# Centred gate weights and a one-hot matrix that carries the row scale, with five engine queues in a new order

## The chip, the cores and the metric

One NeuronCore of a Trainium2 chip runs the kernel. The time is the device time of one execution in microseconds, as the median of several runs. The profiled execution is one further run; its span goes from the first to the last instruction that the profiler shows.

## The reference

Four images of 512 tokens with 512 features go through two gated residual blocks. The first builds, from a 512 x 128 context, a similarity matrix of tokens, keeps in each row the values above the row's 153rd largest, and mixes the normalised input with it:

```
sim = einsum(Q, K) / (sqrt(d) * H)                  # 512 x 512 an image
threshold = top_k(sim, 153)[..., -1:]
A = sigmoid(sim) * (sim >= threshold)
A = (A + A^T) / 2
x = x + tanh(g_xattn) * ((1 - gamma) * layernorm(x) + gamma * A)
```

The second is a mixture of eight experts with two picks a token (gate, softmax over the picks, weights times alpha):

```
n = layernorm(x)
probs = softmax(n @ gate_w);  score, idx = top_k(probs, 2)
h = gelu(n @ fc1_w[e] + fc1_b[e]);  y = h @ fc2_w[e] + fc2_b[e]
x = x + tanh(g_ffn) * sum over the two picks of share * alpha[e] * y
```

Everything is float32. fc1_w and fc2_w are 8 x 512 x 512 each, 16 MB together.

## The kernel before

The program is written with explicit queues: each engine (SyncE for DMA, GpSimd, ScalarE, VectorE, TensorE) has a list of named steps, laid out by hand in one order, and semaphores between them. A queue runs strictly in its order, so a step that waits holds all steps behind it. Steps are named `step(b, t)` for image b and row tile t (128 rows, four an image), or `step(k, e)` for the rows of image k that went to expert e. Images are taken in the order 2, 0, 1, 3, and b counts in that order.

An image goes through these stages.

- Scores. TensorE turns the context (`turn_context`), multiplies by the folded Wq and Wk (`project`, L1596) and makes 512 x 512 scores (`scores`, L1600); ScalarE copies and scales them (`context`, `query`, `scores`).
- Threshold. VectorE takes mean and variance of each row of scores (`sim_stats`) and makes a first guess (`first_guess`, L1014). In three rounds ScalarE (`signs`) and for image 0 also VectorE (`count`) count the scores below the trial threshold, and VectorE moves the trial (`narrow`, L1040). Then `candidates` (ScalarE), `largest` and `threshold` (VectorE) find the value, and TensorE sums the flags in `prove`; VectorE reads the sum into a register in `prove` (L1107) and goes on.
- Mask and first block. ScalarE has made the sigmoid (`squash`, `halve`) and the normalised input (`affine_x`, L719, from `x_stats`, `x_var`, `x_scales` of VectorE and a power on GpSimd). VectorE masks (`mask`), adds (`total`), TensorE transposes the masked matrix (`adjacency`, L1616), VectorE adds that (`add`). `store_x1` of SyncE writes the sum out.
- Second norm and routing. VectorE takes the statistics (`x1_stats`, `x1_var_of`), GpSimd the power (`rstd_of_x1`), VectorE the bias (`norm_bias`) and the normalised rows (`norm`, L1168) into `ab`. TensorE transposes the raw sum (`turn`), ScalarE copies (`turned`), TensorE multiplies by the gate weights (`gate`, L1643) into `logit_ps`, a PSUM tile. `best_two` (L1174) takes off the mean times the column sums of the gate weights (`gate_sum`, from `sum_gate` and `keep_gate_sum`) into `logits`, finds the two largest and their numbers, and makes the one-hot `hot` and `member`. `rank` (TensorE), `shares` and `places` (VectorE) give each row its weights and its place in the lists of its experts.
- Dispatch. GpSimd writes the rows of `ab` to these places in DRAM by eight indirect DMAs an image (`scatter_rows`, L561). SyncE reads them back by expert (`load_rows`, L384, four DMAs each) and reads the rows' numbers and weights (`load_meta`, read by `targets` on VectorE). For the first two experts of image 0 the rows don't take that way: `norm_plain` (ScalarE, L732) makes the normalised rows, `one_hot` (VectorE, L1234) a matrix that picks them, `pick_rows` (TensorE, L1661) multiplies the two, `picked` (ScalarE, L740) copies the result.
- Experts. `turn_rows` (VectorE, L1300) transposes the read rows, `layer1` (TensorE, L1670) 64 or, in pairs of passes, 32 profiled matmuls, `gelu` (ScalarE), `layer2` (TensorE, L1698), `add_bias` (VectorE, L1316, with the row that `load_b2` brought), `weigh` (ScalarE) and `add_result` (GpSimd, L570), an indirect DMA that adds the rows into the output. One of these DMAs waits for the one before. The result rows lie in two buffers for images 0 to 2, so that `add_bias(m)` waits until m - 1 results have been added (`freed`). In the last image the lists are 160 long; the 32 rows behind 128 are done for four experts at once (`tails`, `spread_tokens`, `find_twins`, `merge`, `add_tails`).

TensorE has only one queue, in which the stages of the images are interleaved: scores and masks of image b + 1 and b + 2 stand between experts of image b. `keep_busy` (L1579) is filler, small matmuls whose result nobody reads; `busy_to_threshold` starts it when two tiles of `largest` are done. Weights come expert by expert, two MB each (`load_weights`, L316); two of the eight pairs come after the stores of image 0.

## Time and profile before

| | us |
|---|---|
| median of three runs | 364.29 |
| lowest and highest | 364.28, 367.03 |
| span of the profiled execution | 363.4 |
| TensorE busy in the span | 324.3 |
| VectorE busy | 200.7 |
| ScalarE busy | 165.0 |
| GpSimd busy | 100.1 |

The page of the profile gives busy times, the granted clock of TensorE by slices, the chain of work that ended last, and groups of instructions. The table by stage gives the same for any stretch. The list of waits says which instruction an engine stood before, and which engine and line released it. A timeline gives single or merged instructions: start, duration, engine, line, operation, output and inputs, and in brackets the idle time before and its releaser. Times count from the start of the span. A 128 x 512 instruction of VectorE or ScalarE that stands in a run is shown with some 0.7 us but starts about 0.6 us behind the one before.

### The profile page before, as it was taken

Reading aid. Unit: us, or ns where it says so; the run is one execution under the profiler, and the core shown is the slowest. Engines: PE = TensorE matmul, PEld = TensorE weight load, DVE = VectorE, ACT = ScalarE, POOL = GpSimd, SP = SyncE. Lnnn points to the kernel's source line nnn. Section 1 sums busy time; section 2 is a strip of 40 time slices with the busy share of each in tenths; the row PEclk is TensorE's granted clock in tenths of the full one; section 3 lists DMA queues with packets and bytes.
Section 4 is the critical chain, followed back from the end, with each engine's and each line's share of the span. In section 5 each row is a group of like instructions: output and inputs, shape, how many; then the busy total and the mean of one; then the engine's idle time right before and its main releaser. Section 6 shows DMA issues by size and latency. Waiting matters only on the chain.

```text
span 363.4 us, 6131 instructions
## 1 busy us (share of the span) xinstructions
PE 324.3 (89%) x1937; PEld 232.9 (64%) x1937; DVE 200.7 (55%) x697; ACT 165.0 (45%) x384; POOL 100.1 (28%) x141
## 2 busy tenths in 40 slices
PE   6906899779998999899999989999999999999960
PEld 4402667677764786678778576777785877577610
DVE  0488698887879777898886372636206112311010
ACT  2485515389996746256786222232222213132320
POOL 5001001361111357114307431331733111312031
PEclk9975699899999999999999999999999999999996
DMA  2999989977974696876627587744678854533253
GB/s 91 379 392 369 352 298 331 378 267 139 305 145 123 144 243 231 146 161 183 113 54 181 191 173 135 211 100 81 203 163 149 176 119 104 111 64 87 30 74 46
DMA packets 53636, 65.79 MB, mean 181 GB/s; under 512 B 9792, under 2 KB 28512, under 8 KB 53600
## 3 DMA queue, kind: packets, MB, share of 16 engines
q1 hardware_dynamic: 46144, 47.99, 43.7%
q0 software_dynamic: 7456, 17.37, 24.7%
q8 instruction: 16, 0.26, 0.3%
q14 instruction: 20, 0.16, 0.1%
HBM read 39.56 MB, written 25.78 MB: 180 GB/s over the span
## 4 chain that ended last, share of the span: by engine, by line
PE 50%; issue 18%; DVE 14%; DVEq 5%; DMA 5%; POOL 3%; POOLq 2%; ACT 2%; ACTq 0%
PE ps L1711 21%; PE ps L1684 13%; PE ps L1694 10%; DMA out_rows<-ab,dst 3%; PE ps L1647 2%; POOL xs_rows L566 2%; DMA meta<-xs_rows 2%; DVE top L1087 1%; DVE stats L1012 1%; PE ps L1607 1%; PE ps L1721 1%; PE ps L1627 1%; PE ps L1639 1%; POOLq L530 1%; DVEq L1086 1%
## 5 line engine op out<-in xcount | busy, mean ns | idle before, releaser
L1684 PEld LDWEIGHTS ps<-xgT_r,weights 128*128 128x128 f32 x768 | 87.8, 192 | 8.3 <-issue 6.7
L1684 PE MATMUL ps<-xgT_r,weights 128*128 128x128 f32 x768 | 89.6, 276 | 3.6 <-ACT xgT_r L743 2.0
L1711 PE MATMUL ps<-weights,act_r 128*128 128x512 f32 x192 | 86.3, 595 | 1.5 <-ACT act_r L766 1.5
L580 POOL DMA_INDIRECT out_rows<-ys,dst x24 | 37.9, 1578 | 115.2 <-ACT ys L773 70.0
L1711 PEld LDWEIGHTS ps<-weights,act_r 128*128 128x128 f32 x192 | 34.9, 190 | 38.4 <-issue 36.5
L766 ACT ACTIVATE act_r<-ps,b1T 128x128 f32<-128x128 f32 x96 | 27.1, 365 | 38.9 <-PE ps L1684 38.8
L1694 PEld LDWEIGHTS ps<-sim,weights 128*128 128x128 f32 x256 | 35.2, 190 | 1.9 <-issue 1.7
L566 POOL DMA_INDIRECT xs_rows<-ab,pos x32 | 31.9, 998 | 14.5 <-issue 9.1
L1694 PE MATMUL ps<-sim,weights 128*128 128x160 f32 x256 | 35.6, 299 | 0.0
L773 ACT ACTIVATE ys<-ys,meta 128x512 f32<-128x512 f32 x24 | 17.3, 719 | 31.3 <-DVE ys L1322 31.3
L1322 DVE TENSOR_TENSOR ys<-ps,b_r 128x512 f32<-128x512 f32 x24 | 16.5, 686 | 23.4 <-PE ps L1711 22.0
L1711 PE MATMUL ps<-weights,xb 128*128 128x512 f32 x64 | 28.1, 592 | 0.0
L1322 DVE TENSOR_TENSOR ab<-ps,b_r 128x512 f32<-128x512 f32 x10 | 6.9, 691 | 35.8 <-PE ps L1711 30.0
L692 ACT ACTIVATE ab<-sim,t_now 128x512 bf16<-128x512 f32 x36 | 25.5, 719 | 2.4 <-DVEq L1057 2.3
L580 POOL DMA_INDIRECT out_rows<-ab,dst x8 | 12.3, 1542 | 46.2 <-ACT ab L773 30.3
L1309 DVE STREAM_TRANSPOSE xgT_r<-xg_r 128x512 f32<-128x512 f32 x22 | 15.5, 707 | 12.9 <-PE ps L1684 11.9
L1607 PE MATMUL ps<-ctxT,qT 128*128 128x512 f32 x32 | 20.9, 782 | 0.7 <-ACT qT L677 0.7
L766 ACT ACTIVATE xb<-ps,b1T 128x160 f32<-128x160 f32 x32 | 10.0, 395 | 24.7 <-PE ps L1694 24.7
L1711 PEld LDWEIGHTS ps<-weights,xb 128*128 128x128 f32 x64 | 11.9, 190 | 13.4 <-issue 13.4
L1309 DVE STREAM_TRANSPOSE sim<-sim 128x640 f32<-128x640 f32 x8 | 6.8, 845 | 22.3 <-PE ps L1694 21.1
L1647 PEld LDWEIGHTS ps<-gate_w,x1T 128*128 128x128 f32 x128 | 15.7, 192 | 2.2 <-issue 1.4
L1582 PE MATMUL ps<-ones_b 128*128 128x128 bf16 x136 | 12.0, 260 | 5.5 <-DVE top L1087 3.0
(206 smaller groups left out, 419.0 us busy)
## 6 DMA issues: line engine op xcount, KB each, us to landing
weights<-in_L_ffn_fc_w SPq DMA_DIRECT2D x16, 1024.0 KB, 8.0
b_r<-in_L_ffn_fc_b SPq DMA_DIRECT2D x32, 256.0 KB, 4.1
xg_r<-xs_rows SPq DMA_DIRECT2D x88, 64.0 KB
xb<-in_x SPq DMA_DIRECT2D x4, 1024.0 KB, 7.1
out_rows<-xb SPq DMA_DIRECT2D x4, 1024.0 KB, 5.5
sim<-xs_rows SPq DMA_DIRECT2D x32, 80.0 KB
xs_rows<-weights SPq DMA_DIRECT2D x1, 2064.0 KB, 13.5
xs_rows<-weights SPq DMA_DIRECT2D x2, 516.0 KB, 5.9
```

The lines of the kernel that those rows point to most:

```text
L566: pool.indirect_dma_start(out=xs_rows, out_offset=bass.IndirectOffsetOnAxis(ap=pos[:, g:g + 1], axis=0), in_=ab[:, b % 2, t, :], in_offset ...
L580: pool.indirect_dma_start(out=out_rows, out_offset=bass.IndirectOffsetOnAxis(ap=dst[:, k % 2, e:e + 1], axis=0), in_=result_rows(m), in_of ...
L692: last = act.activation(junk(b, t), score_of(b, t), ACT.Sign, bias=t_now[:, i:i + 1], scale=-1.0, accum_out=cnt[:, i:i + 1])
L766: last = act.activation(to, at, ACT.Gelu, bias=b1T[:, e * IB + i:e * IB + i + 1])
L773: act.activation(result_rows(m), result_rows(m), ACT.Copy, scale=meta[:, k % 2, e, 3:4]).then_inc(ys_ok, 1)
L1309: dve.transpose(to, at.rearrange("p (s k i) -> p k s i", k=KB, i=QUAD)).then_inc(xgT_ok, 1)
L1322: dve.tensor_tensor(result_rows(m), ps[:, 2 + u, :], b2_r[:, u, :], ALU.add).then_inc(y_sb, 1)
L1607: pe.matmul(ps[:, SIDE_BANK + t % 2, :], qT[:, t * P:(t + 1) * P], ctxT[:], start=True, stop=True).then_inc(sim_ps, 1)
L1647: mm = pe.matmul(logit_ps[:, t, :], x1T[:, t % 2, k * P:(k + 1) * P], gate_w[:, k, :], start=(k == 0), stop=(k == KB - 1))
L1684: mm = pe.matmul(ps[:, n % 2, i * P:(i + 1) * P], weights[:, e, 0, h, i * P:(i + 1) * P], rows[:, h * P:(h + 1) * P], start=(h == 0), stop ...
L1694: mm = pe.matmul(at, weights[:, e, 0, h, i * P:(i + 1) * P], rows[:, h * LAST:(h + 1) * LAST], start=(h == 0), stop=(h == KB - 1))
L1711: mm = pe.matmul(ps[:, 2 + m % 2, :], rows, weights[:, e, 1, i, :], start=(i == 0), stop=(i == IB - 1))
```

## The change

Three edits of the arithmetic and a new order of all queues.

1. The gate weights are centred once: `centre_gate` on VectorE subtracts from each column of the gate weights its mean, from the sums that `sum_gate` made. `gate` then multiplies by `gate_c`, which takes the row mean off by itself, and `best_two` reads `logit_ps` directly. `gate_sum` and `logits` go.
2. `norm_plain` only subtracts the row mean, from the new `neg_mean`, and no longer waits for the scale.
3. `one_hot` multiplies the picking matrix by the row's scale (one over the standard deviation), so that `pick_rows` gives the normalised rows.
4. SyncE, GpSimd, ScalarE, VectorE and TensorE run their steps in another order. Two waits move or are new on TensorE (`m_sb` into `project`, `gate_ok` into `gate`), one on ScalarE (`mean_ok` for `bias_ok`).

The edits of the arithmetic, and the parts of the order that the prediction speaks of, queue by queue (SyncE, GpSimd, ScalarE, VectorE, TensorE):

```diff
-            load_b2(0, 1)
+            load_weights(6)
             store_x1(0)
             fill_pads()
-            load_weights(6)
             load_x(2)
-            load_weights(7)
+            load_b2(0, 1)
             load_meta(0)
             load_rows(0, 2)
             load_rows(0, 3)
             fill_ends()
             load_rows(0, 4)
+            load_rows(0, 5)
             load_b2(0, 2)
-            load_rows(0, 5)
             load_b2(0, 3)
-            load_rows(0, 6)
             load_b2(0, 4)
             store_x1(1)
             load_b2(0, 5)
+            load_rows(0, 6)
+            load_weights(7)
             load_rows(0, 7)
+            load_b2(0, 6)
             load_x(3)
-            load_b2(0, 6)
+            load_rows(1, 0)
+            load_rows(1, 1)
             load_b2(0, 7)
+            load_meta(1)
             load_b2(1, 0)
...
             load_b2(2, 6)
+            load_rows(3, 2)
             load_b2(2, 7)
-            load_meta(3)
-            for t in range(3):
-                load_rows(3, t)
             load_b2(3, 0)
             load_rows(3, 3)
+            load_rows(3, 4)
+            load_meta(3)
...
+            add_result(0, 0)
+            add_result(0, 1)
+            add_result(0, 2)
             rstd_of_x1(1)
             add_result(0, 3)
+            scatter_rows(1, 0)
+            scatter_rows(1, 1)
+            scatter_rows(1, 2)
             add_result(0, 4)
-            for t in range(BT):
-                scatter_rows(1, t)
+            scatter_rows(1, 3)
...
+            rstd_of_x1(3)
             add_result(1, 7)
             add_result(2, 0)
-            rstd_of_x1(3)
             add_result(2, 1)
+            scatter_rows(3, 0)
             add_result(2, 2)
+            scatter_rows(3, 1)
+            scatter_rows(3, 2)
+            scatter_rows(3, 3)
             add_result(2, 3)
-            for t in range(BT):
...
-                    act.wait_ge(bias_ok, 1)
+                    act.wait_ge(mean_ok, 1)
                     act.wait_ge(blank, 16)
                     act.wait_ge(sum_ps, 1)
-                act.activation(plain(t), xb[:, 0, t, :], ACT.Identity, scale=xn_scale[:, t:t + 1],
-                               bias=xn_bias[:, t:t + 1]).then_inc(plain_ok, 1)
+                act.activation(plain(t), xb[:, 0, t, :], ACT.Identity, bias=neg_mean[:, t:t + 1]).then_inc(plain_ok, 1)
...
-            scores(2, 2)
             scores(2, 3)
             context(3)
-            for t in range(BT):
-                affine_x(1, t)
-            query(3)
             signs(1, 0)
             picked(0)
             picked(1)
@@ -833,126 +853,140 @@
...
                 dve.drain().then_inc(x1_var, 1)
+                if b == 0:
+                    dve.tensor_scalar(neg_mean[:], mv1[:, :, 0], -1.0, None, ALU.mult).then_inc(mean_ok, 1)
...
                 for t in range(BT):
-                    dve.scalar_tensor_tensor(logits[:, t, :], gate_sum[:], mv1[:, t, 0:1], logit_ps[:, t, :], ALU.mult,
-                                             ALU.add)
+                    dve.max(out=best[:, t, :], in_=logit_ps[:, t, :])
                 dve.drain()
                 for t in range(BT):
-                    dve.max(out=best[:, t, :], in_=logits[:, t, :])
-                dve.drain()
-                for t in range(BT):
-                    dve.max_index(out=best_i[:, t, :], in_max=best[:, t, :], in_values=logits[:, t, :])
+                    dve.max_index(out=best_i[:, t, :], in_max=best[:, t, :], in_values=logit_ps[:, t, :])
...
-                    last = dve.tensor_scalar(xg_r[:, e, t * P:(t + 1) * P], place_no[:], chosen[:, t, e:e + 1], None,
-                                             ALU.is_equal)
+                    last = dve.tensor_scalar(xg_r[:, e, t * P:(t + 1) * P], place_no[:], chosen[:, t, e:e + 1],
+                                             xn_scale[:, t:t + 1], ALU.is_equal, ALU.mult)
...
-            def keep_gate_sum():
+            def centre_gate():
                 dve.wait_ge(sum_ps, 1)
-                dve.tensor_scalar(gate_sum[:], total_ps, -1.0, None, ALU.mult)
-
+                for k in range(KB):
+                    last = dve.scalar_tensor_tensor(gate_c[:, k, :], total_ps, -1.0 / D, gate_w[:, k, :], ALU.mult, ALU.add)
+                last.then_inc(gate_ok, 1)
+
+            x_stats(0, 0)
+            x_stats(0, 1)
+            x_stats(0, 2)
+            x_stats(0, 3)
+            x_var(0)
+            sim_stats(0, 0)
+            x_stats(1, 0)
             coefficients()
+            x_scales(0)
+            x_stats(1, 1)
+            sim_stats(0, 1)
+            sim_stats(0, 2)
+            sim_stats(0, 3)
+            centre_gate()
             first_guess(0)
-            keep_gate_sum()
             count(0, 0)
-            x_stats(0, 1)
             narrow(0, 0)
             count(0, 1)
-            x_stats(0, 2)
             narrow(0, 1)
             count(0, 2)
-            x_stats(0, 3)
-            x_var(0)
             narrow(0, 2)
-            x_scales(0)
-            x_stats(1, 0)
-            for t in range(BT):
-                largest(0, t)
-            x_stats(1, 1)
...
+            total(0, 0)
+            sim_stats(1, 2)
+            total(0, 1)
+            total(0, 2)
+            total(0, 3)
+            add(0, 0)
+            add(0, 1)
+            x_stats(1, 3)
+            add(0, 2)
+            add(0, 3)
+            x1_stats(0, 0)
+            x1_stats(0, 1)
+            x1_stats(0, 2)
+            x1_stats(0, 3)
+            sim_stats(1, 3)
+            first_guess(1)
             x1_var_of(0)
-            x_stats(1, 2)
-            x_stats(1, 3)
+            best_two(0)
             norm_bias(0)
             norm(0, 0)
             norm(0, 1)
-            best_two(0)
             norm(0, 2)
+            sim_stats(2, 0)
+            one_hot(0)
+            sim_stats(2, 1)
             norm(0, 3)
+            gaps(0)
             x_var(1)
-            sim_stats(1, 0)
...
-            sim_stats(1, 3)
-            first_guess(1)
-            for t in range(BT):
-                sim_stats(2, t)
             first_guess(2)
             narrow(1, 0)
-            for t in range(BT):
-                x_stats(2, t)
+            next_places(0)
+            x_stats(2, 0)
+            x_stats(2, 1)
+            narrow(1, 1)
+            x_stats(2, 2)
+            x_stats(2, 3)
             x_var(2)
-            narrow(1, 1)
             x_scales(2)
+            narrow(1, 2)
             targets(0)
             turn_rows(0, 2)
-            narrow(1, 2)
             add_bias(0)
+            add_bias(1)
             turn_rows(0, 3)
+            largest(1, 0)
...
             scores(1, 0)
             scores(1, 1)
+            turn_context(2)
             busy_to_threshold()
+            prove(0)
+            keep_busy(BUSY_MASK)
             scores(1, 2)
-            prove(0)
+            keep_busy(16)
             scores(1, 3)
-            keep_busy(BUSY_MASK)
-            project(2)
             adjacency(0, 0)
             adjacency(0, 1)
+            project(2)
+            turn_b1()
             turn_context(3)
-            keep_busy(16)
             adjacency(0, 2)
             adjacency(0, 3)
...
             pick_rows(0)
-            project(3)
             pick_rows(1)
             layer1(0, 0)
             layer1(0, 1)
             layer2(0, 0)
+            layer2(0, 1)
             layer1(0, 2)
-            layer2(0, 1)
+            project(3)
             layer1(0, 3)
             layer2(0, 2)
             prove(1)
+            layer2(0, 3)
             layer1(0, 4)
-            layer2(0, 3)
...
             layer2(0, 5)
             layer2(0, 6)
             prove(2)
+            scores(3, 2)
+            scores(3, 3)
             layer1(0, 7)
-            layer2(0, 7)
             adjacency(2, 0)
             adjacency(2, 1)
+            layer2(0, 7)
             layer1(1, 0)
             layer1(1, 1)
...
+            layer1(1, 6)
             layer1(1, 7)
             adjacency(3, 0)
+            layer2(1, 6)
             adjacency(3, 1)
-            layer1(2, 0)
             layer2(1, 7)
-            layer2(2, 0)
-            layer1(2, 1)
             adjacency(3, 2)
             adjacency(3, 3)
+            layer1(2, 0)
+            turn(3, 0)
+            layer1(2, 1)
...
-            layer1(2, 3)
+            layer1(2, 4)
             gate(3, 2)
             gate(3, 3)
+            layer2(2, 2)
             layer2(2, 3)
             rank(3)
...
             layer2(2, 6)
-            layer2(2, 7)
             layer1(3, 0)
             layer1(3, 1)
+            layer1(3, 2)
+            layer2(2, 7)
...
+            spread_tokens()
             tails(0)
-            spread_tokens()
-            layer1(3, 4)
+            layer1(3, 5)
             merge(0)
-            layer1(3, 5)
+            layer1(3, 6)
             layer2(3, 4)
             layer2(3, 5)
-            layer1(3, 6)
             layer1(3, 7)
             layer2(3, 6)
             layer2(3, 7)
```

## Rows read from the trace of the kernel before

**Rows 1.** The page, part 1 (busy us, share).
```profile
PE 324.3 (89%) x1937; PEld 232.9 (64%) x1937; DVE 200.7 (55%) x697; ACT 165.0 (45%) x384; POOL 100.1 (28%) x141
```

**Rows 2.** Table by stage: stretch, its length, busy us (instructions) by engine, clock.
```profile
107.00:150.00 43.00, 39.98 (x226) 27.05 (x225) 35.79 (x113) 26.36 (x60) 17.12 (x16) 1.00 0.68 172
...
150.00:230.00 80.00, 78.80 (x505) 60.19 (x504) 54.56 (x178) 39.91 (x99) 27.21 (x22) 1.00 0.66 147
```

**Rows 3.** TensorE's waits from 78 us: us in total, times, longest.
```profile
PE ps L1711 <- ACT act_r L766: 1.5, 2, 1.2
...
PE ps L1684 <- DVE xgT_r L1309: 1.2, 1, 1.2
...
PE ps L1627 <- DVE xb L1149: 1.0, 1, 1.0
```

**Rows 4.** Timeline of VectorE, image 0: start us, duration us, line, operation.
```profile
18.78 0.16 DVE L1025 SCALAR_TENSOR_TENSOR t_now<-dev,mv 128x4 f32<-128x4 f32 x1
...
20.89 0.69 DVE L992 BATCH_NORM_STATS2 statx<-xb 128x6 f32<-128x512 f32 x1
...
33.01 0.17 DVE L1079 COPY_PREDICATED t_now<-under,keep 128x4 f32<-128x4 int32 x1
...
59.32 0.62 DVE L1178 SCALAR_TENSOR_TENSOR logits<-gate_sum,mv,ps 128x8 f32<-128x8 f32 x4
...
60.02 0.37 DVE L1182 MAX8 best<-logits 128x8 f32<-128x8 f32 x4
...
65.84 0.87 DVE L1242 TENSOR_SCALAR xg_r<-place_no,chosen 128x128 f32<-128x128 f32 x4
...
69.35 0.17 DVE L1231 CAST pos<-pos_f 128x8 uint32<-128x8 f32 x1
```

**Rows 5.** Timeline of TensorE; last row from the chain that ended last.
```profile
37.49 4.02 PE L1582 MATMUL ps<-ones_b 128*128 128x128 bf16 x36 [3.00 <-DVE top L1087]
...
44.06 3.23 PE L1582 MATMUL ps<-ones_b 128*128 128x128 bf16 x48
...
66.77 1.23 PE L1666 MATMUL ps<-xg_r,act_r 128*128 128x128 f32 x4 [2.42 <-DVE xg_r L1242]
...
71.95 1.02 PE L1598 MATMUL ps<-ctxT,m_qk 128*128 128x512 f32 x2
...
78.56 7.38 PE L1684 MATMUL ps<-xgT_r,weights 128*128 128x128 f32 x64 [2.02 <-ACT xgT_r L743]
...
85.78 3.60 PE L1711 MATMUL ps<-weights,act_r 128*128 128x512 f32 x8
...
251.47 0.24 PE L1658 MATMUL ps<-member,ones_b 128*128 128x8 bf16 x4
...
279.84 8.69 PE ps L1694 x64
```

**Rows 6.** Table by stage, two short stretches: the granted clock is named after POOL's.
```profile
42.00:44.00 2.00, 2.00 (x6) 0.48 (x5) 0.65 (x2) 0.60 (x1) 0.00 (x0) 0.84 1.04 399
...
66.00:67.00 1.00, 0.23 (x1) 0.24 (x2) 0.99 (x7) 0.60 (x2) 0.00 (x0) 0.77 1.06 408
```

**Rows 7.** Timelines of ScalarE, GpSimd, SyncE and VectorE, in order of time.
```profile
71.48 2.93 ACT L722 ACTIVATE xb<-xb,xa_bias,xa_scale 128x512 f32<-128x512 f32 x4 [4.88 <-DVEq L1008]
...
130.74 1.57 POOL L580 DMA_INDIRECT out_rows<-ys,dst  x1 [4.95 <-ACT ys L773]
...
264.04 0.97 POOL L566 DMA_INDIRECT xs_rows<-ab,pos  x1 [0.30 <-issue]
...
268.31 0.38 SPq L377 DMA_DIRECT2D meta<-xs_rows  x1
...
278.17 0.85 DVE L1309 STREAM_TRANSPOSE sim<-sim 128x640 f32<-128x640 f32 x1 [1.02 <-DMA sim<-xs_rows]
...
345.21 1.54 POOL L580 DMA_INDIRECT out_rows<-ab,dst  x1 [8.50 <-ACT ab L773]
...
350.85 1.54 POOL L580 DMA_INDIRECT out_rows<-ab,dst  x1 [4.10 <-DMA out_rows<-ab,dst]
```

542 lines of the change are left out of this document (296 added, 246 removed).

## The prediction

> **What bounds the kernel now.** I read the page first, then the table by stage, then TensorE's waits, then the timelines of the five engines around each wait. TensorE is busy 89% of the span, but the mean hides two regimes [rows 1]. From 78.56 us, the first expert matmul of `layer1(0, 0)`, it has almost no idle time: 3.0 us of the 43 from 107 on and 1.2 of the 80 behind [rows 2]. What it waited for there is a short list: 1.5, 1.2 and 1.0 us [rows 3], and 2.0 at 78.56 itself, where ScalarE's `picked` came late [rows 5]. So the time is the start of `layer1(0, 0)`, plus TensorE's work behind it, which the change doesn't alter, plus some 4 us of waits, plus the tail. Before 78.56 TensorE mostly waits; the chain there runs through image 0's threshold search, mask, statistics, routing and one-hot matrices, nearly all on VectorE. A microsecond off that chain counts only until another queue, equally late, holds TensorE.
>
> **The small edits.** `best_two` loses four scalar_tensor_tensor instructions, 0.62 us in a run, and a drain, together 0.70 from the start of L1178 to that of L1182 [rows 4]. In return four MAX8 and four index searches read PSUM. No row has either with a PSUM source; the bounds are the 0.09 us step of the SBUF MAX8 and the 0.155 step of the PSUM-reading L1178. Eight times the difference is 0.5 us, so an image gains 0.2 to 0.7. I take 0.2, since L1178 is the nearest row: same shape, same source. With 0.7 all behind it would be 0.5 earlier. The Trainium skill, VectorE: DVE Perf Modes, section "The TRN2 errata", gives a PSUM source 62 cycles more than an SBUF one; eight instructions would be an estimated 0.5 us more. By the page the edit gains 0.2, not 0.7. The one-hot compare gains a second scalar operand (0.87 us for four, [rows 4]): nothing below, and 0.3 above if each cost as much as L1178's extra step. `norm_plain` waits for the mean instead of the scale and bias, and is no longer last: in the new order it ends near 64, before the one-hot matrix that the same matmuls need. `centre_gate` is four instructions like L1178, 0.6 us, in place of one small one, and stands ahead of the first trial threshold. The three new waits (on the gate sums, the mean and the centred weights) are for work that ends at least 2 us earlier in the layout below.
>
> **The front in the new order.** I laid the new queues out with the durations of the trace.
> - Threshold search. Before, the first trial was out at 18.94 and the last at 33.2 [rows 4]. Now four `x_stats`, `x_var`, three of them formerly between the rounds, `x_scales`, two of image 1 and `centre_gate` run ahead of it: the first trial comes near 21.7. Between the rounds only `count` and `narrow` remain, and each former `x_stats` there was 0.6 us [rows 4]: the last trial comes near 33.3. No gain, no loss.
> - Mask. `prove(0)` no longer stands behind a half-clock score matmul: 0.6 us earlier. One `sim_stats` and one `x_stats` put between `total` and `add` cost 1.2. The statistics of x1 start about 0.5 later than before.
> - Routing. `sim_stats(1, 3)` and `first_guess(1)` (2.2 us) stand ahead of `x1_var_of(0)`, so the mean is out near 59.0, later than before, but `best_two(0)` follows at once rather than after two `x_stats`, `norm_bias` and two `norm`. Members near 61.6. The matmuls that it reads (`gate`) end near 58.5, hidden behind the statistics.
> - One-hot matrices. `one_hot(0)` stands behind three `norm` and one `sim_stats` instead of two, two, an `x_var` and `gaps`: 65.3 against 66.7 [rows 4]. `one_hot(1)` ends near 68.5, and TensorE asks for it only at 70.5.
> - `pick_rows(0)` starts at 65.3 instead of 66.77 and I keep its 5.2 us, since it began at half clock after an idle stretch [rows 5, 6]; `project(3)`, 0.9 us in the pipeline [rows 5], no longer divides the two; `pick_rows(1)` follows: ends 74.1.
> - `picked(0)` on ScalarE stood behind four `affine_x(1, ..)` (2.9 us) that waited for VectorE until 71.5 [rows 7]. These are moved behind the first experts; `signs(1, 0)` finds its trial ready since 58, so both copies are done by 74.7.
>
> `layer1(0, 0)` then starts at 74.1 instead of 78.56 [rows 5]: 4.5 us. `project(3)` comes back after `layer1(0, 2)`: minus 0.9, so 3.6 us.
>
> **What holds TensorE next.** `layer2(0, 1)` now comes right behind `layer2(0, 0)`. Its GELU is behind `signs(1, 1)`, the table load, `gelu(0, 0)` and `signs(1, 2)`: near 85.0, wanted at 74.1 plus two `layer1` of 3.6 and a `layer2` of 3.45 (the starts 78.56 and 85.78, and 3.60 less the overlap [rows 5]), 84.75: 0.3 late. `layer1(0, 2)` needs `turn_rows(0, 2)`, which has been moved behind `narrow(1, 2)` (2.5 us); rows are written by the eight scatters of image 0, whose places come 1.1 later than the 69.5 of before [rows 4]. The transpose ends near 89.2, 0.8 after TensorE asks. Left: 2.5 us. Behind `layer1(0, 4)`, `adjacency(1, 2)` waits for `add(1, 0)`, which follows the four `halve` and two late `affine_x`: 1.7 us against 1.0 [rows 3] and two short ones, 0.5 together, before. Left: 2.3.
>
> **The middle.** Before, `layer2(0, 7)` waited 1.2 us for its GELU, TensorE paused 0.3 at a rank (part of the 3.0 of [rows 2]), and `layer1(2, 0)` waited 1.2 for its transpose [rows 3]. In the new order `scores(3, 2)`, `scores(3, 3)` and `adjacency(2, 0)` stand ahead of `layer2(0, 7)` and cover the first; `rank(1)` finds its members; `layer2(1, 7)`, `adjacency(3, 2)` and `(3, 3)`, 4.3 us, are new ahead of `layer1(2, 0)`; by the layout its rows are turned near 209.3 and TensorE asks near 211.4. All three go: 2.7 us. Lead 5.0. The b2 loads, `store_x1` and `load_x` are moved within SyncE's queue and land at least 2 us before their readers by the same laying out; `load_weights(7)` now goes out near 118, needed near 138; in return `load_x(2)` has no 2 MB ahead of it while DMA is full.
>
> **The last image.** `rank(3)` gets `layer1(2, 4)` (3.6 us) ahead of it, so with a lead of 5.0 it ends at 250.3 instead of 251.7 [rows 5]. Places take 1.15, eight scatters of 1.28 (start to start) 10.2, and `add_result(2, 2)`, which before stood behind all eight and now among them, 1.85: the last scatter ends near 263.2 (before 265.0), and SyncE, which went on at 268.3, goes on at 266.5 [rows 7]. It now issues rows ahead of the metadata: issue 2.0, landing 3.0 (as for the rows awaited at 278.17 [rows 7]), transpose 0.85: 272.4. TensorE asks at 279.84 [rows 5] less the 3.4 of `layer2(2, 7)`, which now stands behind, less 5.0: 271.4. With a landing of 2.5 or 3.0 that is 0.5 or 1.0 lost; I take 0.8. The tail is the same chain of accumulating DMAs behind `layer2(3, 6)`; with `layer1(3, 6)` moved ahead of `layer2(3, 4)` the adds of experts 4 and 5 just finish before that of 6 is ready (5.6 us each from issue to issue [rows 7], 11.2 for 4.35 + 2 x 3.45). No term.
>
> Sum against the profiled span: 363.4 - 4.5 + 0.9 + 1.1 + 0.2 - 2.7 + 0.8 = 359.2. The median of the runs is 0.9 above the span, which I carry along: 360.1.
>
> **Rivals.**
> - A, this forecast: 358.3 to 361.7. Chance 0.46, 0.36 of it under 360.65.
> - B, the front's gain comes but each wait saved in the middle returns elsewhere (a hand layout misses some): 364.3 - 2.3 + 0.8 = 362.8, up to 364.5. For it: every queue changes, and the experts have only two row buffers. Against: the idle times of VectorE in the middle are small but exist. Chance 0.22.
> - C, the late pieces near 85, 89, 110 and 271 are all on time: 364.3 - 3.6 - 2.7 - 1.5 = 356.5, to 358.3. Chance 0.14.
> - D, slower. On GpSimd three `scatter_rows(1, ..)` now stand before `add_result(0, 4)`, which before was issued at 130.74, ahead of them [rows 7]. It must wait for image 1's places (near 128.4), then 7.7 us of scatters, then 5.5 of its own: landed 141.6. `add_bias(6)` on VectorE waits for it and is reached near 143; behind it stands `turn_rows(1, 0)`, without which TensorE has nothing. Places later than 129.8 cost time one for one; over 5.6 us late the kernel is slower than before, and at 10 us late it takes 368.7. The same is laid out for images 2 and 3. Chance 0.10.
> - E, the clock. The fillers from 37.49 ran without a gap into the scores, and the granted clock rose from 1.2 to 2.4 GHz within 42 to 44 us [rows 5, 6]. Now `prove(0)` waits some 0.3 us after the fillers' end. If the rise goes late by the whole stretch to the turns, 48 fillers at the pace of the first 36 (0.11 us against 0.067 [rows 5]) cost 2.0 more, and scores, adjacency and projection about 2.3: 364.3. Chance 0.08. The Trainium skill, TensorE: Matmul & The Clock Gate, Part 1, has the throttled state as the default, which activity lifts. By that rule, with which the rise behind the fillers agrees, E is possible.
>
> **Numbers.** About 1% (3.64 us) is what a measurement can tell from no change. Faster by more: 0.36 + 0.14 = 0.50. Within: 0.10 + 0.22 + 0.08 = 0.40. Slower: 0.10. The range 356.5 to 364.5 leaves out D, the low end of C (0.04) and the high end of B and E (0.04).
>
> **What would show it.** Right: `layer1(0, 0)` within 1 us of 74.1; ScalarE no longer releasing it; small waits at 85 and 89 and one of 1 to 2 us at `adjacency(1, 2)`; no wait at `layer2(0, 7)` and `layer1(2, 0)`; `layer1(3, 0)` near 272; TensorE's last expert matmul some 4.2 us earlier. Wrong: a first trial later than 22, a wait of `ys` L1322 for a DMA, or a clock of 0.5 after 44 us.

## The result and the profile after

| | before | after |
|---|---|---|
| median of 4 runs, us | 364.91 | 371.59 |
| lowest and highest | 364.28, 367.03 | 368.83, 375.20 |
| profiled execution, its span | 363.4 | 367.8 |

The ratio is 1.0148, 95% interval [1.0100, 1.0196]: the kernel after is 1 to 2% slower. The ratio leaves out the run of 375.20 as a slow one, since it lies more than 1.5% above the fastest. The four runs of after have mean granted clocks of 0.960, 0.959, 0.934 and 0.950 in the order 368.83, 369.54, 373.63, 375.20 us, so the two slower ones had the lower clocks, though not in strict order. The trace below is that of the run of 369.54.

Busy times of the whole span, from the page of the profile after (in before: [rows 1]):

```profile
PE 322.6 (88%) x1937; PEld 231.9 (63%) x1937; DVE 197.2 (54%) x685; ACT 163.2 (44%) x384; POOL 101.3 (28%) x141
```

TensorE does the same work in 1.7 us less, since more of the front ran at full clock, yet the span is 4.4 us longer: the loss is idle time. (The clock of the front differs from run to run: the kernel before, profiled again as c0 below, has 325.1 us of work on TensorE where the first profile has 324.3.) Its longer waits from 74 us on, from the timeline of TensorE (start, duration, engine, line, operation, tiles; in brackets the idle time and its releaser; rows without a wait and three with 0.33 to 0.43 are left out):

```profile
74.42 7.31 PE L1765 MATMUL ps<-xgT_r,weights 128*128 128x128 f32 x64
83.29 3.70 PE L1792 MATMUL ps<-weights,act_r 128*128 128x512 f32 x8 [1.57 <-ACT act_r L778]
87.32 3.70 PE L1792 MATMUL ps<-weights,act_r 128*128 128x512 f32 x8 [0.33 <-ACT act_r L778]
92.26 3.81 PE L1765 MATMUL ps<-xgT_r,weights 128*128 128x128 f32 x32 [1.24 <-issue]
...
113.36 1.23 PE L1706 MATMUL ps<-ident,ab 128*128 128x128 f32 x8 [1.23 <-DVE xb L1183]
...
129.63 0.20 PE L1735 MATMUL ps<-member,before 128*128 128x8 bf16 x2 [0.31 <-DVEq L1228]
131.06 3.81 PE L1765 MATMUL ps<-xgT_r,weights 128*128 128x128 f32 x32 [0.93 <-issue]
...
153.66 7.41 PE L1765 MATMUL ps<-xgT_r,weights 128*128 128x128 f32 x64 [0.88 <-DVE xgT_r L1341]
...
188.88 1.06 PE L1728 MATMUL ps<-gate_c,x1T 128*128 128x8 f32 x8 [1.53 <-ACT x1T L743]
...
301.09 3.70 PE L1792 MATMUL ps<-weights,xb 128*128 128x512 f32 x8 [0.55 <-ACT xb L778]
```

With the three left out they make 9.7 us, where before had 2.0 at `layer1(0, 0)` [rows 5] and 4.2 behind it (the listed ones of [rows 3], one of them 0.23, and two more of 0.24 and 0.34). `layer1(0, 0)` starts at 74.42: the front's gain came. By `layer2(0, 2)` TensorE is 0.5 us later than before. Behind `gate(2, 3)` (188.88) the clock fell; the table by stage (length, busy time of each engine with counts, granted clock, DMA share, GB/s):

```profile
188.00:190.70 2.70, 1.82 (x16) 1.82 (x17) 2.04 (x10) 2.25 (x6) 0.00 (x0) 1.00 0.81 151
190.80:194.10 3.30, 3.30 (x18) 3.30 (x17) 2.76 (x13) 1.14 (x4) 1.18 (x1) 0.50 0.65 173
194.20:210.00 15.80, 15.80 (x85) 9.73 (x84) 10.28 (x34) 8.35 (x19) 8.34 (x9) 1.00 0.56 136
```

At half clock the `layer1` there took 5.45 us, where the same step in e2 below took 3.82 at full clock: 1.6 us.

### The profile page after: what moved, and what is told of

Read it like the earlier page. It is cut to its first block, busy times and chain, and to the rows that moved or that the text cites. A ratio compares the mean times of both kernels' runs of the same rounds, so it can differ in the third digit from the quotient of the medians.

```text
span 367.8 us, 6116 instructions
## 1 busy us (share of the span) xinstructions
PE 322.6 (88%) x1937; PEld 231.9 (63%) x1937; DVE 197.2 (54%) x685; ACT 163.2 (44%) x384; POOL 101.3 (28%) x141
## 4 chain that ended last, share of the span: by engine, by line
PE 47%; DMA 12%; DVE 11%; issue 8%; ACT 7%; POOL 5%; DVEq 3%; SPq 3%; POOLq 2%; ACTq 1%
PE ps L1792 18%; PE ps L1765 13%; PE ps L1775 6%; DMA out_rows<-ys,dst 5%; POOL xs_rows L568 4%; ACT ab L705 3%; DMA out_rows<-ab,dst 3%; DMA xb<-in_x 2%; PE ps L1728 2%; PE ps L1659 2%; PE ps L1686 2%; POOLq L554 1%; SPq L397 1%; POOL out_rows L582 1%; DVE xg_r L1071 1%
## 5 line engine op out<-in xcount | busy, mean ns | idle before, releaser
L1765 PEld LDWEIGHTS ps<-xgT_r,weights 128*128 128x128 f32 x768 | 89.6, 195 | 8.1 <-issue 6.4
L1765 PE MATMUL ps<-xgT_r,weights 128*128 128x128 f32 x768 | 91.5, 279 | 3.0 <-issue 2.2
L582 POOL DMA_INDIRECT out_rows<-ys,dst x24 | 38.7, 1612 | 115.0 <-ACT ys L785 63.6
L1686 PE MATMUL ps<-ctxT,qT 128*128 128x512 f32 x32 | 18.9, 706 | 11.9 <-ACT qT L690 11.9
L1792 PEld LDWEIGHTS ps<-weights,xb 128*128 128x128 f32 x64 | 11.9, 190 | 14.8 <-issue 13.4
L1659 PE MATMUL ps<-ones_b 128*128 128x128 bf16 x136 | 13.6, 264 | 8.6 <-DVE top L1121 6.1
L743 ACT COPY x1T<-ps 128x512 f32<-128x512 f32 x16 | 9.3, 590 | 25.5 <-PE ps L1718 17.3
L1659 PEld LDWEIGHTS ps<-ones_b 128*128 128x128 bf16 x136 | 10.7, 119 | 12.7 <-issue 12.1
L1728 PEld LDWEIGHTS ps<-gate_c,x1T 128*128 128x128 f32 x128 | 15.5, 192 | 3.4 <-ACT x1T L743 2.0
```

The source lines that it names most:

```text
L582: pool.indirect_dma_start(out=out_rows, out_offset=bass.IndirectOffsetOnAxis(ap=dst[:, k % 2, e:e + 1], axis=0), in_=result_rows(m), in_of ...
L1659: pe.matmul(ps[:, 3, 0:P], ones_b[:], ones_b[:], start=True, stop=True)
L1686: pe.matmul(ps[:, SIDE_BANK + t % 2, :], qT[:, t * P:(t + 1) * P], ctxT[:], start=True, stop=True).then_inc(sim_ps, 1)
L1728: mm = pe.matmul(logit_ps[:, t, :], x1T[:, t % 2, k * P:(k + 1) * P], gate_c[:, k, :], start=(k == 0), stop=(k == KB - 1))
L1765: mm = pe.matmul(ps[:, n % 2, i * P:(i + 1) * P], weights[:, e, 0, h, i * P:(i + 1) * P], rows[:, h * P:(h + 1) * P], start=(h == 0), stop ...
L1792: mm = pe.matmul(ps[:, 2 + m % 2, :], rows, weights[:, e, 1, i, :], start=(i == 0), stop=(i == IB - 1))
```

## The experiments

All are given as start of the same step of TensorE minus its start in the kernel before [rows 5], both from the start of their span, in us (negative: earlier), each from its one profiled run, and as median of runs with the median of before beside it on the same chip. The steps are chosen so that the same work lies ahead of them; only at `layer1(0, 0)` before, c0, both e3, h2, h9 and g1 have done `project(3)` (0.9 us) and the others not. e1, e4, g2 to g4, k1 and k2 stand in the text alone.

| kernel | layer1(0,0) | layer1(0,3) | layer2(0,4) | layer1(1,1) | layer2(3,7) | median, before |
|---|---|---|---|---|---|---|
| after | -4.1 | +0.5 | +0.3 | +1.9 | +5.1 | 371.59, 364.91 |
| c0_before_again | -1.8 | -0.2 | -1.2 | -0.9 | +1.6 | 365.88 (one run), 363.68 |
| e2_rstd_first | -4.2 | +0.5 | +0.2 | +1.5 | +5.5 | 370.64, 366.15 |
| e3_arith_alone | -0.1 | -0.1 | 0.0 | +0.6 | 0.0 | 363.61, 366.15 |
| e3_arith_again | -1.9 | -0.3 | -1.3 | -1.5 | -2.1 | 362.99, 364.68 |
| h1_new_front | -2.5 | +3.7 | +4.9 | +4.7 | +3.8 | 370.91, 363.68 |
| h2_new_rest | -0.8 | -0.2 | +0.3 | +2.7 | +6.8 | 371.05, 363.68 |
| h3_front_repaired | -4.9 | -3.7 | +2.4 | +3.1 | +2.3 | 368.28, 363.68 |
| h4_fill_later | -4.4 | -3.6 | +0.8 | +4.6 | +3.8 | 366.89, 364.84 |
| h5_image1_first | -3.4 | -2.4 | -1.2 | +3.5 | +2.9 | 366.46, 364.84 |
| h9_taken_parts | -0.1 | -0.1 | +0.4 | +5.2 | +4.4 | 369.20, 364.68 |
| g1_arith_power_first | -1.7 | 0.0 | -1.1 | +2.2 | +1.9 | 365.02, 364.71 |

The row of c0 is the kernel before itself, profiled once more. It sets the measure: a difference of one trace to another of up to some 1.8 us can be the run and not the kernel. In c0, e3_arith_again and g1 `layer1(0, 0)` ran at half clock (5.44 us instead of 3.81), so that their early start there was gone at the next step: `layer1(0, 1)` starts at 82.06, 81.94 and 82.18, in before at 82.21, in after at 77.99. A profiled run can also lie off the median of its kernel (h1: 368.22 against 370.91, its fastest), and its trace then explains only part of the median.

**Arithmetic against order.**

```diff
-                act.activation(plain(t), xb[:, 0, t, :], ACT.Identity, scale=..., bias=xn_bias[...])
+                act.activation(plain(t), xb[:, 0, t, :], ACT.Identity, bias=neg_mean[...])
```

e3 has all edits of the arithmetic, this one among them, with the queues of before; e4 has none of them, with the queues of after.

> Kernel before with only the arithmetic edits (gate_c from centre_gate, neg_mean in norm_plain, scale in one_hot, best_two straight from PSUM), all queues in the old order. Theory of this document: best_two gives 0.7 on the path and takes nothing (four MAX8 from PSUM took 0.39 in after, 0.37 from SBUF in before), centre_gate costs 0.2 to 0.4 ahead of the first trial, the two one_hot 0.25 each more: within 0.5 us of before. Rival M (the arithmetic costs the time, for example because norm_plain or the new waits hold an engine): slower than before by 2 us or more.

> Kernel after with the old arithmetic (gate_sum, logits, norm_plain with scale and bias and the wait for the bias, one_hot without scale), all queues in the new order. Order is the cause: within 1.5 us of after (norm_plain stands early on ScalarE and now waits for norm_bias(0), near 62 us, some 2 us later than the mean; scores(2, 2) behind it are late by that). Rival M: at least 2 us faster than after.

e3: 363.61 against 366.15, ratio 0.9940 [0.9905, 0.9975]. e4: 374.19, ratio 1.0141 [1.0069, 1.0213], like after. The order is the cause, and the arithmetic alone is a gain. In the trace of e4 the clock was at half from 133.6 to 137.0 and from 191.6 to 198.4. The arithmetic a second time, and the kernel before once more for its trace:

> The kernel of e3_arith_alone once more, with more rounds and beside h9_taken_parts. e3_arith_alone measured 0.994 of before, [0.9905, 0.9975], but its trace starts layer1(0, 0) and all later stages within 0.15 us of the trace of before save one wait of 1.2 that became 0.5. If the ratio was a property of the kernel: again 0.992 to 0.997. If it was the spread of before on that chip: 0.998 to 1.001.

> The kernel before, unchanged, for a trace from the same chip as these runs. Its stages should lie within 0.3 us of the trace shown; if its start is later (the first loads), that explains why arithmetic alone measured 2 us below it in the median but not in the two traces.

Ratio 0.9954 [0.9921, 0.9988]: the gain holds in two measurements, both on the same chip. Where it comes from the traces don't settle. This run and c0 match in clock up to 214 us: `layer1(0, 6)` waited 0.55 in c0 and not at all here (members of image 1 earlier), 0.9 us by `layer2(0, 5)`; at `layer1(2, 0)` 2.04 became 0.54. But the first pair, e3_arith_alone and before, shows no gain at `layer1(0, 6)` (it waited 0.40 and 0.34), because there the add ahead of image 1's norm took 7.2 us to land instead of 6.5; at `layer1(2, 0)` it waited 0.52 against 1.21. At the front the arithmetic brings nothing that lasts: `one_hot(0)` is earlier, but `picked(0)` waits longer behind `affine_x(1, ..)`.

Behind that wait of 2.04 in c0 the kernel before itself lost the clock, from 214.5 to 217.9; the timeline of TensorE and the table by stage of c0:

```profile
213.49 5.46 PE L1684 MATMUL ps<-xgT_r,weights 128*128 128x128 f32 x32 [2.04 <-DVE xgT_r L1309]
```
```profile
214.60:217.80 3.20, 3.20 (x17) 3.20 (x17) 3.12 (x6) 0.00 (x0) 1.70 (x1) 0.50 0.87 203
```

In the first profile of before the same step waited 1.21 and the clock did not fall.

**The chain through GpSimd's queue.** In after, ScalarE's `weigh(0, 7)` stands behind `signs(3, 1)`; from the timeline of GpSimd in after and, last line, of VectorE:

```profile
170.99 1.53 POOL L582 DMA_INDIRECT out_rows<-ys,dst  x1 [16.10 <-ACT ys L785]
177.42 1.54 POOL L582 DMA_INDIRECT out_rows<-ys,dst  x1 [4.90 <-DMA out_rows<-ys,dst]
178.44 1.61 POOL L553 TENSOR_TENSOR rstd_x<-var_x,neg_half 128x4 f32<-128x4 f32 x1
182.83 0.23 POOL L558 TENSOR_SCALAR var<-mv 128x4 f32<-128x4 f32 x1 [2.78 <-issue]
```
```profile
182.72 0.23 DVE L1038 TENSOR_SCALAR xs_tmp<-rstd_x,coef 128x4 f32<-128x4 f32 x1 [4.50 <-POOLq L554]
```

The power `rstd_x` runs at 178.44, but its signal comes only behind the drain of the queue, when the add issued at 177.42 has landed (182.1); VectorE goes on at 182.72. `add_bias(9)`, `weigh(1, 1)` and the copy for `gate(2, 3)` stand behind that. Two repairs:

```diff
 e1, ScalarE
+            weigh(0, 7)
             turned(2, 0)
             signs(3, 1)
             gelu(1, 1)
-            weigh(0, 7)
 e2, GpSimd
+            rstd_of_x(3)
+            rstd_of_x1(2)
             add_result(1, 0)
-            rstd_of_x(3)
-            rstd_of_x1(2)
```

> Kernel after, with one ScalarE step moved: weigh(0, 7) ahead of turned(2, 0), signs(3, 1) and gelu(1, 1) instead of behind them. Theory G (GpSimd's queue): the late weigh(0, 7) holds add_result(0, 7) to 171.0, add_result(1, 0) waits for its DMA until 177.4, the two powers rstd_of_x(3) and rstd_of_x1(2) stand behind it, VectorE's x_scales(3) waits 4.5 us, gate(2, 3) 1.5 us, and the granted clock falls behind that wait. Then here add_result(0, 7) is issued near 165, the powers run near 175, x_scales(3) waits under 0.5, gate(2, 3) does not wait, no half clock near 191 to 194: 3 to 3.5 us faster than after, near 366 as a median of runs of after near 369.5. Rival F (the wait at gate(2, 3) is only TensorE's own small slip and the clock falls anyway): within 1 us of after. Rival M (arithmetic): no change.

> Kernel after, with two GpSimd steps moved: rstd_of_x(3) and rstd_of_x1(2) ahead of add_result(1, 0) instead of behind it; ScalarE as in after, so add_result(0, 7) stays near 171. Theory G: the powers run while the DMA of add_result(0, 7) is under way (variances are out at 174.7), end near 177, x_scales(3) waits under 0.5, gate(2, 3) does not wait, the clock stays: 3 to 3.5 us faster than after, as the other repair. If only the late weigh counts and not the queue behind it: no gain. Rivals F and M: within 1 us of after.

e1: 372.92 (368.54 to 375.96) against 366.15; the add went out at 167.1, but the powers stayed behind `add_result(1, 0)`, issued at 175.74. The first power ran at 177.56, and its signal came at 182.4, behind the landing of that add at 181.8: no cure. e2: 370.64, ratio 1.0113 [1.0056, 1.0170]. Here the chain is cured: `x_scales(3)` does not wait, `gate(2, 3)` neither, no fall of the clock there, and `layer1(1, 7)` stands 3.4 us earlier than in after (206.27, 209.70). Then it is given back:

```profile
219.85 0.63 PE L1706 MATMUL ps<-ident,ab 128*128 128x128 f32 x4 [1.66 <-DVE xb L1183]
234.99 3.84 PE L1765 MATMUL ps<-xgT_r,weights 128*128 128x128 f32 x32 [1.25 <-DVE xgT_r L1341]
```
```profile
218.41 0.71 DVE L1341 STREAM_TRANSPOSE xgT_r<-xg_r 128x512 f32<-128x512 f32 x1 [7.25 <-DMA xg_r<-xs_rows]
```

VectorE (second fence) waits 7.25 us at `turn_rows(2, 0)` for the rows of image 2, and `add(3, 1)` behind it holds TensorE (first fence). The scatters of image 2 began at 198.0 there, at 193.6 in before.

**New front, new rest.**

> New arithmetic; TensorE, ScalarE and VectorE in the new order up to the first experts (layer2(0, 0), gelu(0, 1), narrow(1, 0)), then the order of before; SyncE and GpSimd in the order of before. affine_x(1, ..) and query(3) stay behind the first experts, project(3) behind layer1(0, 2). Theory R (the rest of the new order costs the time, the new front itself gives nothing lasting): layer1(0, 0) near 74.4, the lead of 4.2 us gone by 100 us (late gelu(0, 0), and rows of the third expert 3 us later than before, since the scatters start at 72.9 instead of 69.9), then as before: within 1.5 us of the kernel before, no half clock between 80 us and the end. Rival L (the front's lead survives under the old rest): 3 us or more faster than before. Rival Q (the new front harms image 1's search, and the rest only passes it on): 3 us or more slower than before, as after.

> The complement: new arithmetic; TensorE, ScalarE and VectorE in the order of before up to layer1(0, 0), candidates(1, 0) and add_bias(0), then the new order; SyncE and GpSimd in the new order. Theory R: the rest loses its 4 to 7 us here too: layer1(0, 0) near 78.6, waits near adjacency(1, 2), layer1(1, 0) and gate(2, 3), total 4 us or more slower than before. Rival Q: within 1.5 us of before.

h1: ratio 1.0209 [1.0153, 1.0266]; h2: 1.0171 [1.0112, 1.0230]. Either half alone costs as much as the whole, so neither theory R nor rival Q of these expectations stands as put. In h1 `gelu(0, 0)` is 1.57 us late, and `layer1(0, 2)` waits 3.37 for `turn_rows(0, 2)`, whose rows landed at 91: the lead is gone and 3.7 us more by `layer1(0, 3)`. In h2 the waits are those of after from 107 on, `gate(2, 3)` and the fall of the clock (191.9 to 195.3) among them.

**The front repaired.**

```diff
 h3, TensorE
             scores(2, 1)
+            rank(0)
             keep_busy(12)
             scores(2, 2)
-            rank(0)
 h4, SyncE, on top
             load_rows(0, 3)
-            fill_ends()
             load_rows(0, 4)
...
             load_rows(0, 6)
+            fill_ends()
 h5, on top, ScalarE (and VectorE alike)
-            signs(2, 1)
             squash(1, 3)
...
             halve(1, 3)
+            signs(2, 1)
```

> As h1_new_front, with what held the new front taken away: rank(0) ahead of the fillers and scores(2, 2); all four sim_stats(2, ..) behind places(0); narrow(1, 0) and narrow(1, 1) ahead of the statistics of image 2; narrow(1, 2), targets(0) and turn_rows(0, 2) ahead of x_scales(2); project(3) between layer2(0, 1) and layer1(0, 2). If the front's gain was lost to these places: one_hot(0) ends near 65, the scatters start near 70, layer1(0, 0) near 73, no wait over 0.5 us for gelu(0, 0), layer1(0, 3) near 91 to 92.5 (before 96.3), and 2 to 4 us of it last to the end: 2 to 4 us faster than before. If image 1's search sets the time from 113 on whatever comes before (rival): the wait before adjacency(1, 2) grows by what was gained and the time is within 1 us of before.

> h3_front_repaired with one SyncE step moved: fill_ends, three DMAs of 3.1 MB that stood between load_rows(0, 3) and load_rows(0, 4), behind load_rows(0, 6). In h3_front_repaired the rows of expert 4 landed at 104.6 and layer1(0, 4) waited 4.86 us, then the clock fell for 3.4 us. Theory B (this burst of DMA, which starts only when the last scatter of image 0 has landed, takes the front's gain): turn_rows(0, 4) does not wait for a DMA, layer1(0, 4) starts near 100.4, the lead of 3 us or more over the kernel before lasts to adjacency(1, 0) near 108, and of it 2 to 3.5 us to the end: 361 to 362.5 where the kernel before has 364. Rival A (image 1's search holds adjacency(1, 2) anyway): the wait there grows to 3 us or more, within 1 us of before.

> h4_fill_later with image 1's mask put first: signs(2, 1) on ScalarE behind halve(1, ..) instead of ahead of squash(1, 3); on VectorE largest(1, ..) ahead of narrow(2, 0), narrow(2, 1) behind total(1, 3). If what is left of h4_fill_later's lead is lost before adjacency(1, 2): that wait goes, 1 us more is kept than in h4_fill_later. If image 2's search comes late by it (rival): a new wait before prove(2) or adjacency(2, 0), no gain over h4_fill_later.

h3: 368.28, ratio 1.0114 [1.0041, 1.0187]. The front does what was wanted (a lead of 4.9, still 3.7 at `layer1(0, 3)`), and runs into DMA; VectorE, then TensorE:

```profile
104.61 0.71 DVE L1341 STREAM_TRANSPOSE xgT_r<-xg_r 128x512 f32<-128x512 f32 x1 [4.40 <-DMA xg_r<-xs_rows]
```
```profile
105.42 5.29 PE L1765 MATMUL ps<-xgT_r,weights 128*128 128x128 f32 x32 [4.86 <-issue]
```

Ahead of these rows stood `fill_ends`, three writes of 3.1 MB together, issued from 88.2 on, the largest of which (2 MB) took 13.4 us to land. h4: 366.89, ratio 1.0050 [1.0017, 1.0083]: the wait of 4.86 is 0.37, theory B is right there. But the expected 361 to 362.5 did not come: waits of 0.72, 2.07 (`gelu(0, 3)`), 0.43, 0.82 and 1.63 follow, and the clock was at half from 107.5 to 110.9 and from 134.8 to 138.2. h5: 366.46, ratio 1.0068 [1.0027, 1.0108], no nearer to before than h4. Its lead at `layer2(0, 4)` is 1.2 us; then the table by stage of h5:

```profile
111.00:120.00 9.00, 7.61 (x42) 4.90 (x40) 8.31 (x26) 8.11 (x17) 1.86 (x2) 1.00 1.05 350
120.20:130.40 10.20, 10.20 (x32) 7.10 (x32) 4.44 (x26) 4.88 (x12) 2.67 (x2) 0.50 0.53 114
```

Some 5 us are lost there, in gates, scores and transposes at 1.2 GHz.

**Only the moves that answer a wait.**

> Kernel before with the new arithmetic and only those moves that answer a wait of TensorE in the trace of before: signs(2, 1) behind halve(1, ..), largest(1, ..) ahead of narrow(2, 0), narrow(2, 1) behind total(1, 3) (wait of 0.98 before adjacency(1, 2)); turn_rows(0, 6) right behind best_two(1) (0.34 behind rank(1), and the 0.9 of scores(3, 3) that is taken away from there); scores(3, 3) between layer1(0, 7) and layer2(0, 7), its copy on ScalarE behind gelu(0, 7) (1.23 before layer2(0, 7)); layer2(1, 7) ahead of layer1(2, 0) and layer2(2, 0) behind layer1(2, 1) (0.5 to 1.2 before layer1(2, 0)). If these waits are the kernel's own slack: 1.5 to 3 us faster than the arithmetic alone, near 361 where before has 364; the gain ahead of 152 us is bounded by the rows of image 1, which landed at 151.3. If the chain of image 1 to its rows sets the time there (rival): layer1(1, 0) waits for what was gained, and only some 0.5 us stay. If the clock falls as in the new orders: a half-clock stretch after 80 us in the profile.

369.20, ratio 1.0138 [1.0092, 1.0184], with no fall of the clock behind 80 us. Every wait that was aimed at is there again or was passed on: `adjacency(1, 2)` 1.56 (0.98 in before), `rank(1)` 1.48 (0), `prove(2)` 0.92 (0), `layer1(0, 7)` 0.73 (0), `layer1(1, 0)` 1.22 (under 0.2). Only those before `layer2(0, 7)` (0.37) and `layer1(2, 0)` went. The cause of the large one is on GpSimd:

```profile
119.68 1.55 POOL L580 DMA_INDIRECT out_rows<-ys,dst  x1 [11.53 <-ACT ys L772]
120.71 0.84 POOL L556 TENSOR_SCALAR var<-mv 128x4 f32<-128x4 f32 x1
126.75 1.04 POOL L558 TENSOR_TENSOR xn_scale<-var,neg_half 128x4 f32<-128x4 f32 x1 [5.20 <-issue]
```

`rstd_of_x1` has a drain between its two instructions. The add issued at 119.68 took 6.8 us to land, 126.5, and the second instruction starts 0.27 later. In before the same steps stand as follows, again on GpSimd:

```profile
115.47 1.55 POOL L580 DMA_INDIRECT out_rows<-ys,dst  x1 [7.18 <-ACT ys L773]
```
```profile
118.46 0.23 POOL L556 TENSOR_SCALAR var<-mv 128x4 f32<-128x4 f32 x1 [1.44 <-DVEq L1161]
122.22 1.04 POOL L558 TENSOR_TENSOR xn_scale<-var,neg_half 128x4 f32<-128x4 f32 x1 [3.54 <-issue]
```

There the add took 6.5 us, in after (116.65, 123.62) 6.7: the second instruction starts 0.25 and 0.27 behind the landing. In image 3 it comes later, 1.4 us behind the landing in before (233.24, 234.65) and 0.7 in after (235.15, 235.86), but in no trace ahead of it. The drain lasts at least until the accumulating DMA ahead of it has landed. So image 1's norm hangs on when `weigh(0, 2)` is run. Ahead of that on ScalarE stands `signs(2, 2)`, which waited 4.02 us for `narrow(2, 1)`, a step that this kernel had moved back.

**The power ahead of the add.**

```diff
 GpSimd, in e3 (g1), e2 (g2), h5 (g3) and h9 (g4)
+            rstd_of_x1(1)
             add_result(0, 2)
-            rstd_of_x1(1)
```

> Arithmetic alone (e3) with one GpSimd step moved: rstd_of_x1(1) ahead of add_result(0, 2). Theory P (the drain inside rstd_of_x1 lasts until the DMA issued ahead of it has landed): the power runs at the statistics, near 117.5, ends near 118.7 instead of 122.1; norm(1, 0) near 119.5 instead of 122.5; members of image 1 some 2 us earlier (gate(1, 3) near 123.5 bounds them), no wait at layer1(0, 6), none at layer1(1, 0): 0.5 to 1.5 us faster than e3, near 362 where before has 364.7. Rival V (VectorE's queue sets it): norm(1, ..) as before, within 0.3 us of e3.

> Kernel after with three GpSimd steps moved: rstd_of_x1(1) ahead of add_result(0, 2), rstd_of_x(3) and rstd_of_x1(2) ahead of add_result(1, 0). Theory P: the power of image 1 ends near 120 instead of 124.7, members near 127.5 instead of 129.5, no waits before rank(1), layer1(0, 6) and layer1(1, 0) (0.31, 0.93, 0.88 in after), and scatter_rows(1, ..) 2 us earlier; 2 us faster than e2_rstd_first unless image 2's rows (218.4 there) take it back; then the wait before adjacency(3, 2) and layer1(2, 3) grows by as much. Rival V: within 0.5 us of e2_rstd_first.

> h5_image1_first with rstd_of_x1(1) ahead of add_result(0, 2) (in h5 the add went out at 118.07 and the power at 125.12, 6 us after the statistics). Theory P: the power ends near 120.2, members 4 us earlier, the lead of 1.2 us that h5 had at 114 lasts to 152 and to the end: 2 us or more faster than h5, 362.5 to 363.5 where before has 364.7. Rival V: as h5, 366.5. Rival K (the half-clock stretch from 120 to 130 of h5 comes from the fast stretch of transposes and gates itself): again a half-clock stretch of 3 us or more there, and 2 to 5 us lost to it.

> h9_taken_parts with rstd_of_x1(1) ahead of add_result(0, 2). Theory P: the power that ran at 126.75 runs near 119.5, members near 128 instead of 132, rank(1) does not wait (1.48), prove(2) and layer1(1, 0) wait less (0.92, 1.22): 3 to 4.5 us faster than h9_taken_parts, 365 to 366 where h9 had 369.2. Rival V: within 1 us of h9_taken_parts.

The drain is shown. GpSimd in g1:

```profile
117.38 0.23 POOL L556 TENSOR_SCALAR var<-mv 128x4 f32<-128x4 f32 x1 [10.64 <-DVEq L1171]
117.93 1.04 POOL L558 TENSOR_TENSOR xn_scale<-var,neg_half 128x4 f32<-128x4 f32 x1 [0.32 <-issue]
```

The second instruction follows 0.55 us behind the first, and as closely in the three others. The time is not won:

| | median | ratio to before | its base |
|---|---|---|---|
| g1 | 365.02 | 1.0000 [0.9966, 1.0035] | e3: 362.99, 0.9954 |
| g2 | 379.19 | 1.0407 [1.0339, 1.0476] | e2: 370.64, 1.0113 |
| g3 | 367.65 | 1.0063 [1.0029, 1.0096] | h5: 366.46, 1.0068 |
| g4 | 369.11 | 1.0110 [1.0045, 1.0174] | h9: 369.20, 1.0138 |

In g1 the add that now waits goes out at 119.9 instead of 115.2, each further one waits for the one before, the scatters of image 1 stand behind two of them, and the rows come later: TensorE in g1,

```profile
152.34 9.04 PE L1696 MATMUL ps<-xgT_r,weights 128*128 128x128 f32 x64 [2.08 <-DVE xgT_r L1317]
```

where e3_arith_again waited 0.28; the clock fell at 153.2, for 3.4 us. In g4 the waits before `rank(1)`, `prove(2)` and `layer1(1, 0)` went (0, 0, 0.41), as expected, but the clock was at half from 123.6 to 133.8. In g3 it was at half from 120.9 to 131.1, as its rival K said (in h5 from 120.2 to 130.4): the power's time did not matter to that. In g2 it was at half from 122.3 to 132.5 and from 241.7 to 245.1, which is some 7 us of its 8 over e2.

**The quiet stretch and the rows of image 2.**

```diff
 k1, TensorE (on e2)
-            layer2(0, 4)
             turn(1, 0)
...
             gate(1, 1)
+            layer2(0, 4)
 k2 on top: VectorE
+            shares(2)
+            places(2)
             turn_rows(1, 6)
...
             turn_rows(1, 7)
-            shares(2)
-            places(2)
 and GpSimd
             scatter_rows(2, 1)
-            add_result(1, 3)
             scatter_rows(2, 2)
             scatter_rows(2, 3)
+            add_result(1, 3)
```

> e2_rstd_first (after with rstd_of_x(3) and rstd_of_x1(2) ahead of add_result(1, 0)) with one TensorE step moved: layer2(0, 4) from ahead of turn(1, 0) to behind gate(1, 1), so that the stretch of transposes, gates and scores from 111 to 125 us is broken by 3.5 us of expert product. Theory C (that quiet stretch brings on the fall of the clock near 120 to 132, in about half of the runs): no run of the slow group (373 us and more), all between 367 and 371, no half clock between 115 and 140 in the profile. Rival (the fall comes from elsewhere): two groups as in after. The gates come no earlier, so the routing of image 1 and the rest are as in e2 (368.0 of span) in either case.

> k1_product_between with image 2's dispatch brought forward: shares(2) and places(2) on VectorE ahead of turn_rows(1, 6), largest(3, 2), largest(3, 3) and turn_rows(1, 7); on GpSimd all of scatter_rows(2, ..) ahead of add_result(1, 3). Theory Q (the rows of image 2 took e2's gain): scatters start near 195.5 instead of 198.0 and end 4 us earlier, turn_rows(2, 0) at 214.5 instead of 218.4, the waits before adjacency(3, 2) (1.66) and layer1(2, 3) (1.25) go: 2.5 to 3 us faster than k1. Rival (VectorE is full there and passes it on): the threshold of image 3 comes later and prove(3) or adjacency(3, 0) waits, within 1 us of k1.

k1: 374.56 (371.76 to 378.66), ratio 1.0289 [1.0234, 1.0344]: theory C in this form is refuted. The product had covered waits; without it in its place `turn(1, 0)` and `turn(1, 2)` wait 0.47 and 1.36, and the clock was at half from 121.0 to 127.8. In k2, same queue of TensorE, from the table by stage:

```profile
107.00:115.30 8.30, 6.59 (x52) 5.67 (x51) 8.13 (x14) 6.62 (x16) 1.51 (x1) 1.00 0.27 34
115.40:125.70 10.30, 9.38 (x35) 7.18 (x34) 6.47 (x29) 5.86 (x11) 2.81 (x3) 0.50 0.96 257
```

k2: 372.35, ratio 1.0217 [1.0165, 1.0269], 2.2 us under k1. The scatters of image 2 start at 198.3 (k1: 203.3), and `turn_rows(2, 0)` runs at 216.4 without a wait (k1: 222.2, behind 5.78). The waits before `adjacency(3, 3)` (1.66 in e2, 0.19 in k1) and `layer1(2, 3)` (1.16 in k1) are gone, and a new one of 1.00 stands at 204. Between the two traces k2 had 1.2 us already ahead of image 2's rows; the moved dispatch itself brought some 0.4 by `layer2(2, 0)` and 1.0 more at `layer2(3, 1)`. So theory Q has its mechanism shown, while the size (2.5 to 3 expected, 2.2 between the medians) can't be put down to it alone.

## Why the prediction was wrong

The forecast was 360.1 with a range to 364.5; it came out 371.6. The sign was wrong, and so was the mechanism: the sum took every step brought forward as a gain that lasts, and priced nothing that the moved queues would hold up in turn.

The step that failed is the term for the middle, 2.7 us saved from `layer2(0, 4)` on. The runs showed 4.8 us lost there instead (+0.3 to +5.1 in the table), 1.6 of it by the clock, and h2 with the new rest alone is slower by as much (1.0171). One chain of it is shown: GpSimd's power stands behind an add whose DMA it has to let land. The second failed term is what holds TensorE behind the front, 1.1 us in the sum and 3.1 measured.

In the terms of the trace, 359.2 was forecast for the span and 367.8 came: 2.6 us of the difference had arisen by `layer2(0, 4)`, 6.7 behind it, and the tail gave 0.7 back. Of the other 2.9 us, 2.1 lie between the profiled run and the median and 0.8 between span and run time; they stay open. Step by step:

- **Small edits.** Right in sign, and under-rated. MAX8 took a mean of 160 ns from PSUM (156 from SBUF in before), FIND_INDEX8 166 (161), the two-scalar compare 342 (281): reading PSUM cost next to nothing, so `best_two` gained its 0.7 rather than 0.2. The Trainium skill, VectorE: DVE Perf Modes, section "The TRN2 errata", lets a PSUM source cost 62 cycles more; these rows do not show it. Image 1 got 0.9 us by `layer2(0, 5)` in one pair (e3_arith_again against c0) and nothing in the other (e3_arith_alone against before), a term that the sum did not have. e3 as a whole gains 0.5%.
- **The front.** 74.1 forecast, 74.42 measured, but by two errors that cancel, which is luck: `rank(0)` (64.17) stands behind `scores(2, 1)`, filler and `scores(2, 2)`, the first two in a stretch at half clock (61.0 to 64.4), so the first one-hot matrix was done at 67.1, not 65.3; and `pick_rows(0)` ran at full clock in 3.7 us, not 5.2. The expected signs "within 1 us" held and said nothing of the places, out at 72.5 instead of 70.65.
- **What holds TensorE next.** 1.1 us forecast, 3.1 measured (1.57, 0.33, 1.24), so with `project(3)` nothing was left at 100 us. The term that failed is the lateness of VectorE's `narrow(1, 0)` (its signal let ScalarE go on at 77.75 instead of 75.2) and of the dispatch: the first scatter began at 72.89, in before at 69.86. I had laid out TensorE's start 4.5 us earlier and not asked which of its feeders were moved by as much. None was. h3 shows the next one, the filling DMAs, which no term had.
- **The middle.** This is the term that failed most. 2.7 us were to be saved. The wait before `layer2(0, 7)` went from 1.2 to 0.34 and that before `layer1(2, 0)` went; the 0.3 at the rank became 0.31 and 0.93, and 0.43, 0.88 and 1.53 us are new. From +0.3 at `layer2(0, 4)` TensorE went to +5.1 at its last `layer2`, 1.6 of it by the clock. Two of these waits are traced: the 1.53 at `gate(2, 3)` to the adds and the power on GpSimd (e2 takes it away), and what came back in e2 to the later rows of image 2 (k2). For the others the cause stays open.
- **Rival D** had the right mechanism, GpSimd's order and the DMA that accumulates, at the wrong place: I asked only for `add_bias`, which waits for the DMA by its semaphore, not for what a drain behind it holds. VectorE's waits for it grew as that rival said (in before there is one such wait of `ys`, of 0.2); from the list of waits of after, with their sum in us, their number and the longest:

```profile
DVE ys L1354 <- DMA out_rows<-ys,dst: 12.7, 4, 4.9
DVE xgT_r L1341 <- DMA xg_r<-xs_rows: 12.6, 5, 4.2
DVE xs_tmp L1038 <- POOLq L554: 6.4, 2, 4.5
```

- **Rival E** looked for the clock at 42 to 44 us, where after was back at full clock early; so was c0, at 40.4, so this is the run and not the change. It fell at 190.7 instead, and in other layouts at 105 to 137, 153, 192 and 242. A chance of 0.08 for one place was too little for a mechanism with many.
- **Rival B**, "each wait saved returns elsewhere", is what happened, but its ceiling of 364.5 assumed that waits come back at most at their old size. h9 shows that they come back larger.
- **Signs.** Of the three that would show it wrong, two did: `ys` waited for a DMA, and the clock stood at 0.5 after 44 us. The second was no sign at all, since it holds for the kernel before as well (66.5 to 70.0; c0 at 57.5, 77.9 and 214.5). The first trial was at 21.3, as laid out.
- **The last image.** The 0.8 us before `layer1(3, 0)` did not come, since TensorE came to it late itself (280.4).

The range was too narrow since it was built from single waits. One reading that fits, though no run shows it by itself, is that the gate into the middle is a ring: norm, members, scatter, rows, expert, add, and two row buffers. h1, h2, h9 and g1 each move one part and lose more than they aimed at.

What stays open: how much of after's median, 371.59 against the profiled 369.54, is the clock. e1, g2, after and e2 have the same 9.44 us of TensorE's work in the 11 us from 111 on; the clock fell at 122.3 in e1 and g2 and not in after or e2. None of the five profiles with TensorE's order of before beyond 100 us and its sources untouched (before, c0, both e3, g1) shows a fall from 100 to 150 us, but g1 had one at 153.2 and c0 one at 214.5, so an order that keeps the clock is not shown. The slower runs of after have the lower clocks, but no trace.

The best kernel found is that of e3, arithmetic alone: 0.9940 and 0.9954 of before.

## What to carry to other kernels

In a queue laid out by hand, a step brought forward is worth only what its slowest feeder is brought forward; list the feeders of the next three steps (GELU, rows, buffers) with their new times before counting the gain. Change one engine's queue at a time, and separate arithmetic from order: here the one gained 0.5%, and the order lost 1.4% by itself (e4) and about 2% against the kernel with the arithmetic alone. A short wait of the matrix engine can be where other queues catch up, and taking it away can cost more than it had.

## What the runs showed of the hardware

- A drain on GpSimd behind an indirect DMA lasts at least until that DMA has landed: in image 1 the next instruction came 0.25 to 0.27 us behind landings that took 6.5, 6.7 and 6.8 us, in image 3 some 0.7 (after) to 1.4 us (before) behind. With no DMA under way the same two instructions are 0.39 to 0.55 us apart. The profile books the idle time as "issue" (3.54 in before, 0.32 in g1).
- The granted clock fell from 2.4 to 1.2 GHz in loaded stretches too, behind waits of TensorE of 1.5 to 2.1 us (after 190.7 behind 1.53, c0 214.5 behind 2.04, h4 107.5 behind 2.07, g1 153.2 behind 2.08; also h2 191.9, h4 134.8, g2 241.7), at some 1.6 to 1.7 us each, and some 5 us in the stretch of transposes and gates between 115 and 134; behind others (1.57 at 83.3 in after, 1.66 at 219.9 in e2, 3.37 at 92.0 in h1) it did not. The Trainium skill, TensorE: Matmul & The Clock Gate, Part 1, says that the monitor runs freely and does not start with the kernel; that the same work at the same time fell in e1 and not in after agrees with it.
- Rows read in pieces of 64 KB landed later behind large writes in SyncE's queue. In after, those issued ahead of `fill_ends` (three writes, 3.1 MB together), at 85.3 to 86.9, landed after 2.1 to 2.4 us, and those issued right behind it, at 92.3 to 98.1, after 6.1 to 10.6 us.
